# A graph network layer pair on one core: the convolution weights' sizes spread by a matmul, four tiles' high parts made on GpSimd, the encoder's bias loaded sooner

## The reference

```python
h = relu(layernorm(x))                                  # 1250 x 1024
h = sigmoid(h @ wenc.T + benc)                          # encoder, 1250 x 500
msgs = (h @ conv_weight)[src] * edge_weight[:, None]
agg = segment_sum(msgs, dst)                            # sum over the edges
x = x + (agg + h @ lin_weight.T) @ wdec.T + bdec
h = relu(layernorm(x))
h = h @ W.T + b
x = x + normalised segment_sum of h over the edges and self loops
```

## Time and profile before

| | |
|---|---|
| median of 3 runs | 455.63 us |
| the profiled execution's own time | 455.52 us |
| its span, first to last instruction | 453.7 us |
| PE busy | 444.1 us (98%) |
| DVE busy | 301.2 us (66%) |
| ACT busy | 237.4 us (52%) |
| POOL busy | 41.3 us (9%) |
| granted TensorE clock, mean | 0.996 |

### The profile page before, as it was taken

One profiled execution on the slowest core, in us unless ns is written; L12 is line 12 of the kernel. 1 busy time (PEld: TensorE's weight loads), 2 busy tenths in 40 slices (PEclk: granted clock), 3 DMA queues, 4 the chain that ended last, 5 costly groups with the idle time before them and its releaser, 6 DMA issues.

```text
span 453.7 us, 8837 instructions
## 1 busy us (share of the span) xinstructions
PE 444.1 (98%) x3202; PEld 332.8 (73%) x3202; DVE 301.2 (66%) x604; ACT 237.4 (52%) x452; POOL 41.3 (9%) x63
## 2 busy tenths in 40 slices
PE   6999998999999999999999999999999999999997
PEld 4999988978775465469888878888889844444454
DVE  5999895976864243864767776938471657567652
ACT  6987996657769552234244444658463622222220
POOL 2611200000000000000000000464600000000000
PEclk9999999999999999999999999999999999999999
DMA  7950958299457899045800006151758004323433
GB/s 288 306 175 2 173 87 145 70 317 317 143 162 138 265 79 325 3 124 186 302 13 1 1 0 228 53 186 46 287 213 293 1 7 167 129 92 140 156 119 111
DMA packets 48399, 66.37 MB, mean 146 GB/s; under 512 B 25793, under 2 KB 35024, under 8 KB 46820
## 3 DMA queue, kind: packets, MB, share of 16 engines
q1 hardware_dynamic: 48036, 65.39, 48.5%
q0 software_dynamic: 320, 0.39, 0.4%
HBM read 43.62 MB, written 16.77 MB: 133 GB/s over the span
## 4 chain that ended last, share of the span: by engine, by line
PE 84%; ACT 4%; DVE 4%; DMA 4%; SPq 2%; issue 1%; ACTq 0%; DVEq 0%
PE bank L1587 21%; PE bank L1588 21%; PE bank L1589 20%; PE bank L1603 19%; DMA benc_c<-benc 3%; PE bank L1712 2%; DMA h16T<-x 1%; SPq L696 1%; PE bank L1714 1%; ACT h0T L1027 1%; ACT stage L1076 1%; ACT h L979 1%; ACT cnt L1073 1%; DVE stats L1190 1%; DVE h0T L1310 1%
## 5 line engine op out<-in xcount | busy, mean ns | idle before, releaser
L1603 PE MATMUL bank<-a,h_hi 128*128 128x256 f16 (+3 forms) x400 | 85.5, 270 | 0.0
L1603 PE MATMUL bank<-a,h_lo 128*128 128x256 f16 (+3 forms) x400 | 85.5, 270 | 0.0
L1587 PE MATMUL bank<-right,left 128*128 128x512 f16 (+1 forms) x148 | 54.4, 367 | 0.0
L1588 PE MATMUL bank<-right,left 128*128 128x512 f16 (+1 forms) x148 | 54.4, 367 | 0.0
L1589 PE MATMUL bank<-right,left 128*128 128x512 f16 (+1 forms) x148 | 54.4, 367 | 0.0
L1152 ACT CAST left<-zs 128x512 f16<-128x512 f32 x35 | 21.5, 617 | 60.3 <-PE bank L1589 60.3
L1572 DVE SCALAR_TENSOR_TENSOR x<-bank,dis_u,x 128x512 f32<-128x512 f32 (+2 forms) x37 | 26.7, 722 | 34.2 <-PE bank L1589 34.2
L1587 PE MATMUL bank<-h0T,we 128*128 128x256 f32 (+3 forms) x144 | 41.4, 287 | 1.0 <-DVE h0T L1308 1.0
L1603 PEld LDWEIGHTS bank<-a,h_hi 128*128 128x128 f16 (+1 forms) x400 | 38.9, 97 | 4.2 <-issue 0.3
L1603 PEld LDWEIGHTS bank<-a,h_lo 128*128 128x128 f16 (+1 forms) x400 | 39.1, 98 | 3.8
L1587 PE MATMUL bank<-unit,g 128*128 128x500 f16 (+3 forms) x120 | 40.8, 340 | 0.0
(11 more groups left out here) (191 smaller groups left out, 978.2 us busy)
## 6 DMA issues: line engine op xcount, KB each, us to landing
whole<-w SPq DMA_DIRECT2D x7, 1024.0 KB, 7.8
adj_scratch<-stage SPq DMA_DIRECT2D x50, 125.0 KB, 3.5
right_scratch<-right SPq DMA_DIRECT2D x5, 1024.0 KB, 4.0
right<-right_scratch SPq DMA_DIRECT2D x5, 1024.0 KB, 4.8
h<-x SPq DMA_DIRECT2D x9, 512.0 KB, 6.7
x<-x SPq DMA_DIRECT2D x9, 512.0 KB, 5.4
out<-x SPq DMA_DIRECT2D x18, 256.0 KB
w_tile<-w SPq DMA_DIRECT2D x8, 512.0 KB, 4.9
```

What stands on the lines that cost most here:

```text
L1587: pe.matmul(o, lhs[0], rhs[0], start=first, stop=False, skip_group_check=True)
L1588: pe.matmul(o, lhs[0], rhs[1], start=False, stop=False, skip_group_check=True)
L1603: ins = pe.matmul(o, h1[i][0:n, k, 128 * f:128 * (f + 1)], moving, start=(k == 0 and part == 0 and i == 0), stop=(k == T - 1 and part == p ...
```

## The change

Three edits come together.

1. **Sizes by a matmul.** The detour through DRAM goes: `limit_row`, both SP steps, and the memset of `sizes`. In its place PE multiplies the 128 sums, broadcast along the free axis, by the identity, which puts all of them on every partition of a bank, and DVE takes the maximum from there. The size of wc stands at (1, 1) instead of (2, 1), the scale at (3, 0) instead of (4, 0), and the cuts of wc at (3, 1), (3, 3), (4, 0) and (4, 1) instead of (4, 1) to (4, 3).
2. **High parts on POOL.** For tiles 6 to 9 ACT runs only the pass that writes `h0`; POOL copies `h0` to the high part, and DVE's split waits for that copy. Norm 8 moves from (2, 2) to (2, 1), norm 9 to (2, 2), and split and turn 9 from (3, 0) to directly behind split and turn 8.
3. **Bias sooner.** The DMA of `benc_c` is issued after x's tile 1 and the edge weights, ahead of tile 2, instead of last of the opening loads.

Besides, one of the eight sizes of layer 1's weights moves from beside the first slice to beside the second, and `bounds` from (1, 5) to (1, 7) of the second slice.

```diff
-        (2, 0): [("split", 7), ("turn", 7)] + fifth[1:], (2, 1): [("size", "wc")], (2, 2): both(turn(3)) + [("norm", 8)],
-        (2, 3): [("norm", 9), ("split", 8), ("turn", 8), ("limits", "out")],
...
+        (2, 0): [("split", 7), ("turn", 7)] + fifth[1:], (2, 1): [("norm", 8)], (2, 2): both(turn(3)) + [("norm", 9)],
+        (2, 3): [("split", 8), ("turn", 8), ("split", 9), ("turn", 9), ("spread", "wc")],
...
-            if (n, k) == (1, 5):
+            if (n, k) == (1, 7):
                 steps += [("bounds",)]
...
-            if n == 1 and k in (1, 2, 3):
-                steps += [("size", "w1", KD - 4 + k)] + [("load", "w1", KD - 2 + k)] * (k == 1)
+            if n == 1 and k in (1, 2, 3, 4):
+                steps += [("size", "w1", KD - 5 + k)] + [("load", "w1", KD - 3 + k)] * (k < 3)
...
                 if t == 1:
                     sp.dma_start(ew_raw[:], nat_w).then_inc(ew_in, 16)
+                    sp.dma_start(benc_c[:], benc).then_inc(benc_in, 16)
...
+                elif s[0] == "norm" and s[1] >= 2 * BY_DMA:
+                    t = s[1]
+                    n = tile_rows(t)
+                    pool.wait_ge(relu_ready, t + 1)
+                    if t >= 2 * BY_DMA + 2:
+                        pool.wait_ge(turned[t - 2], 32)
+                    elif t == 2 * BY_DMA + 1:
+                        pool.wait_ge(ew_sized, 1)
+                    nc.gpsimd.tensor_copy(x16[t % 2][0:n, 0, :], h0[t % XRING][0:n, :]).then_inc(split_hi, 1)
...
-                        nc.scalar.activation(x16[t % 2][0:n, 0, :], h0[t % XRING][0:n, :], ACT.Relu, bias=nbias[0:n, t:t + 1],
-                                             scale=rstd[0:n, t:t + 1])
...
-                    dve.wait_ge(relu_ready, t + 1)
+                    dve.wait_ge(split_hi, t - 2 * BY_DMA + 1)
...
-                    dve.wait_ge(limits_in, 16)
-                    link(v.tensor_reduce(limits[:, 0:1], all_limits, AX, ALU.max))
+                    g = ("spread", "wc")
+                    acc_done(dve, g)
+                    v.tensor_reduce(limits[:, 0:1], bank[banks_of[g]][:, 0:P], AX, ALU.max).then_inc(bank_free, 1)
+                    read_done(dve, g)
...
+                if s == ("spread", "wc"):
+                    pe.wait_ge(sizes_ready, 1)
+                    pe.matmul(take(s)[:, 0:P], sizes[:].broadcast_to([P, P]), ident[:], start=True, stop=True,
+                              skip_group_check=True).then_inc(acc_ready, 1)
```

More of the change, by code:

```diff
@@ L182, in schedule @@
     beside = {
-        (1, 0): turn(2)[:2] + fourth[1:3] + turn(2)[2:], (1, 1): fourth[3:], (1, 2): [("norm", 6)] + fifth[:1], (1, 3): [("norm", 7), ("split", 6), ("turn", 6)],
-        (2, 0): [("split", 7), ("turn", 7)] + fifth[1:], (2, 1): [("size", "wc")], (2, 2): both(turn(3)) + [("norm", 8)],
-        (2, 3): [("norm", 9), ("split", 8), ("turn", 8), ("limits", "out")],
-        (3, 0): [("split", 9), ("turn", 9)], (3, 1): [("limits", "in")], (3, 2): both(turn(4)),
-        (4, 0): [("limits", "scale")], (4, 1): cut_wc[:1], (4, 2): cut_wc[1:3], (4, 3): cut_wc[3:],
+        (1, 0): turn(2)[:2] + fourth[1:3] + turn(2)[2:], (1, 1): fourth[3:] + [("size", "wc")], (1, 2): [("norm", 6)] + fifth[:1], (1, 3): [("norm", 7), ("split", 6), ("turn", 6)],
+        (2, 0): [("split", 7), ("turn", 7)] + fifth[1:], (2, 1): [("norm", 8)], (2, 2): both(turn(3)) + [("norm", 9)],
+        (2, 3): [("split", 8), ("turn", 8), ("split", 9), ("turn", 9), ("spread", "wc")],
+        (3, 0): [("limits", "scale")], (3, 1): cut_wc[:1], (3, 2): both(turn(4)), (3, 3): cut_wc[1:2],
+        (4, 0): cut_wc[2:3], (4, 1): cut_wc[3:],
     }
@@ L192, in schedule @@
     dense += [("load", "wl")] + [("g", t) for t in range(4)] + mix(cut_wl, [("g", t) for t in range(4, T)]) + opening[:2]
-    for k, s in enumerate([("g", 2), ("g", 4), ("g", 6), ("g", 8), opening[0]]):
+    for k, s in enumerate([("g", 2), ("g", 4), ("g", 6), ("g", 8)]):
         i = dense.index(s) + 1
@@ L332, in build @@
             bank_for(("s", s[1], s[2]), *dense)
-        elif s[0] in ("t", "e", "g", "z"):
+        elif s[0] in ("t", "e", "g", "z") or s == ("spread", "wc"):
             if not by_dma(s):
@@ L358, in build @@
             frees[s[1:]] = len(frees)
+        elif s == ("limits", "scale"):
+            frees["spread", "wc"] = len(frees)
     nth = {(p, b): p * NB + b for p in range(NP) for b in range(NB)}
@@ L419, in build @@
         minus_half = small("minus_half", [P, 2], F32)
-        sizes = small("sizes", [P, 2], F32)
+        sizes = small("sizes", [P, 1], F32)
         ew_sizes = small("ew_sizes", [EP, 1], F32)
@@ L605, in build @@
         relu_ready = sem("relu_ready")
+        split_hi = sem("split_hi")
         split_ready = sem("split_ready")
@@ L753, in _ @@
                                  bound_row.rearrange("q i -> (q i)").unsqueeze(0).broadcast_to([P, 2 * P])).then_inc(bounds_in, 16)
[L754 to L760, removed]
                 elif s == ("load", "wc"):
@@ L895, in _ @@
                     nc.gpsimd.memset(cnt[:, :, NODES:NODESP], 0.0).then_inc(blank, 1)
-                    pool.wait_ge(blank, 1)
-                    nc.gpsimd.memset(sizes[:], 0.0).then_inc(size_blank, 1)
                 elif s[0] == "var":
@@ L991, in _ @@
                     loaded(act, "wc", 0)
-                    act.wait_ge(size_blank, 1)
-                    nc.scalar.activation(wc_abs[:], wc_raw[:], ACT.Abs, accum_out=sizes[:, 0:1]).then_inc(sizes_ready, 1)
+                    nc.scalar.activation(wc_abs[:], wc_raw[:], ACT.Abs, accum_out=sizes[:]).then_inc(sizes_ready, 1)
                 elif s[0] == "degree":
```

15 lines of the change are left out of this document (2 added, 13 removed).

## The result

The changed kernel takes 456.25 us, median of 20 runs (455.62 to 457.58); the kernel before, on the same chip, 455.00 us, median of 20 (453.98 to 456.07). The ratio is 1.003, interval 1.0022 to 1.0037: slower by 0.3%. The forecast was 457.0 us, slower, and its mechanism is what the trace shows. The profiled execution of the changed kernel took 455.73 us, of which 453.9 are its span.

What follows compares the result with a forecast made beforehand. PE, busy 444.1 of 453.7 us, bounds the kernel. Delays of 3.25 us less 1.8 us of waits removed give +1.5 on 455.5: 457.0 us, range 453.0 to 459.2 (456.1 to 459.0 for the forecast alone).

Steps and rivals of the forecast that it cites:

- The bias: Opening loads: bias DMA issued at about 2.4 instead of 6.85 us; PE's wait goes, 0.25 us earlier from 31.6 on.
- The sizes and the two DMAs: Pass over wc moves into ScalarE's idle time, the DMAs were nobody's wait, added matmul stands where PE waits: nothing.
- SyncE's long row of turns: Both tiles' turns, over 5 us, ahead of the DMAs of windows 10 to 13: between 0 and +1.5, taken as 0.
- The copy, 1.2 us, and the hold: Each GpSimd copy of 128x1024 takes 1.2 us and holds VectorE's instructions with two SBUF inputs for that long.
- VectorE 2.15 us late: Copies 6 and 7 at 42.0 and 46.0 us, less 0.26 idle, delay the variance of tiles 8 and 9 by 2.15.
- ScalarE's wait of 4 us, e(3,0) +2.15, e(3,2) +3.25: ScalarE waits before tile 8's relu pass, delaying e(3,0); copy 9 and both splits then delay hot windows and e(3,2).
- What comes back, -1.8: PE's later waits go: block 4's `h0T` -1.0, the hot window at 78.9 -0.4, the cuts of wc -0.4.
- The third slice, slack used: Moving `bounds` delays the third slice's load some 4.2 us, landing at 203.5; 1.4 us slack: nothing, up to +0.5.
- Rival A: GpSimd's copies don't hold VectorE, or only at times; -2.2 to -2.5 us, 453.2 us, faster; chance 0.25.

Runs made afterwards that it cites:

- the zeros: Changed kernel with GpSimd writing zeros by memset into the high parts of tiles 6 to 9 instead of copying: ratio 0.9966 to before, 453.57 us.
- the second row of the table: Kernel before with only the load of the encoder's bias issued sooner: ratio 1.0006 to before (0.9994 to 1.0018).
- norms back, ScalarE: Changed kernel with norms 8 and 9 and split 9 at their old steps and high parts made by ScalarE: 0.9957 to before, 453.10 us.

## Why the prediction was right, step by step

*The bias, -0.25.* The wait in the trace went, but it was one execution's: the time shows nothing (1.0006; 1.0028 against 1.0030).

*The sizes and the two DMAs, 0.* The pass over wc and the matmul cost nothing. The DMAs were worth up to 0.8 us by the trace, some 0.4 by the time, which is at the edge of the noise. I had looked for them among PE's waits; they stood in the queue ahead of the windows, behind ScalarE's wait of 1.56 us, which I had named and left without a price. SyncE's long row of turns, which I had feared there, cost little: ScalarE waited 0.32 us for a window's DMA at 73.89.

*The copy, 1.2 us, and the hold.* 1.04 us undisturbed. The hold on VectorE, argued from one add in the earlier trace rows, is shown by the zeros that don't hold it. The Trainium skill (SBUF — State Buffer, Who interferes with whom) draws the line where these two kernels show it: reading SBUF holds, only writing doesn't (0.28 and 0.41 us against 1.12 and 1.26). The Trainium skill (GPSIMD Engine Reference, 4.1 Engine selection), by which I had estimated 1.0 us, agrees with the 1.04 measured.

*VectorE 2.15 us late.* 1.52: the first copy took 0.84 (1.12 less 0.28), the second 0.94 by the split's wait, less the idle 0.26. The term was one of size: I had each copy at its whole 1.2 us.

*ScalarE's wait of 4 us, e(3,0) +2.15, e(3,2) +3.25.* 3.60; +1.74; +2.48. In distances from block 2's first transpose e(3,0) is 2.01 us later and e(3,2) 2.75.

*What comes back, -1.8.* Against the trace of before 2.3 us come back, all of it by the second product g(1). But 1.0 of my 1.8, block 4's `h0T`, was a wait of the one profiled execution and no standing cost: the same code with another opening (the second row of the table) doesn't have it. Against that row 1.7 us come back all the same, 0.2 ahead of e(4,0), 0.5 at the hot window and 0.9 by the products with wc, where I had 0.4 and 0.4: a wait that the list gives as 0.38 or 0.40 us lengthens the distance by 0.5 or 0.65. So in distances the change is 2.74 - 1.72 = 1.0 us, where I had 3.25 - 1.8 = 1.5, and the time says 1.25. That the sum came so near is in part luck: the losses were 0.5 us too large, and what comes back was right in sum with one term that isn't there and others too small. Of the miss of 0.75 us 0.5 is the base: the profiled execution took 455.52, and the median of 20 is 455.00.

*The third slice, slack used.* As predicted: ScalarE stands 1.27 us for the raw piece and starts at 202.77 (201.24 before), PE takes it at 206.23 without a wait (206.08 before).

*Rival A* (copies that don't hold VectorE): the kernel with zeros is that case. It is about 1.5 us faster than before, where I had 2.3, and ScalarE's wait is 2.06 us, where I had 2.

The prediction named the coupling (a late variance that nobody minded before, and tile 8's pass now in front of it), but not what each part costs by itself. Measured against the fastest kernel (norms back, ScalarE), the copies with the norms in their old places cost 0.5 to 0.8 us, and the new places with an instruction that holds nobody 0.4 to 0.5 (0.9966 against 0.9957, and the last column). Copies and new places together cost 2.8 to 3.3. But the new places with ScalarE's own passes cost as much (1.0030), in the trace by PE's wait of 1.57 us for `stage` and the fall of the clock behind it. So neither part has a price of its own: the new order is cheap only when the high parts cost neither ScalarE nor VectorE anything, and the copies are cheap only where no engine stands for the late variance. Even with the variance on time ScalarE waits 2.06 us in the new place; the copies make it 3.60, and this reaches e(3,0) in full.

## What to carry to other kernels

Before an instruction that waits is moved ahead on an in-order engine, set its new place against the time at which what it waits for is ready, and count what is queued behind it: one step put back was worth 2.2 us here, while the four passes of 1.14 us that ScalarE was spared were worth nothing, since the fastest kernel kept them. A copy given to GpSimd was paid for here by VectorE where it ran instructions with two inputs in SBUF; put such copies where VectorE waits or runs instructions with one input. And take a wait from one profile as a standing cost only if a second execution with another opening has it too.

## What the runs showed of the hardware that I had not expected

GpSimd's copy can be the one that is held: started at 45.80 (in the changed kernel) amid two-input instructions of VectorE without a gap, it took 3.14 to 3.33 us in six traces, not 1.04, and VectorE's instructions kept their lengths. It ended 0.9 us after VectorE had stopped or gone on to statistics with one input. A memset at the same place took 0.95. And in one trace a wait of PE of 1.57 us, from 62.4 us on, was followed by a fall of the granted clock to 0.50 for some 3 us, and the stretch from e(3,1) to e(3,2) took 1.0 us longer; the waits of up to 0.6 us of the changed kernel between 60 and 70 us, and the one of 1.0 at 74 us in the kernel before, were followed by no fall.
